# A twelve-layer transformer kernel on one core: the last layer's norms and residual, and the way attention's value sums are turned back

## What is computed

```
norm = maximum(linalg.norm(x, axis=-1), 1e-12);  rms_norm = x / norm * 128 ** 0.5 * gamma
light = gelu(rms_norm(x, light_gamma) @ light_w1 + light_b1) @ light_w2 + light_b2
s = einsum('bnd,d->bn', x, routing_token);  scores = coor_descent(s, k, 50 steps)
heavy = gelu(rms_norm(x, heavy_gamma) @ heavy_w1 + heavy_b1) @ heavy_w2 + heavy_b2
out = light + heavy * (score of the position, made of the descent)
```

## Time and profile before

| | |
|---|---|
| runs | 756.26, 756.54, 758.40 us; median 756.54 |
| the profiled execution | 757.45 us, span of its instructions 755.7 us |
| busy, share of the span | PE 79%, PEld 52%, DVE 64%, ACT 33%, POOL 16% |
| mean granted TensorE clock | 0.879 |
| the chain of work that ended last, share by engine | PE 70%, DVE 21%, POOL 4%, ACT 3%, issue 2% |
| attention's loops, five layers | turns of about 3.1 to 4.0 us, all on the chain that ended last |
| L3f, from L1106 of group 0 | 708.74 to 755.7 us |

### The profile page before, as it was taken

One profiled execution on the slowest core, in us unless ns is written; L12 is line 12 of the kernel. 1 busy time (PEld: TensorE's weight loads), 2 busy tenths in 40 slices (PEclk: granted clock), 3 DMA queues, 4 the chain that ended last, 5 costly groups with the idle time before them and its releaser, 6 DMA issues.

```text
span 755.7 us, 10867 instructions
## 1 busy us (share of the span) xinstructions
PE 597.1 (79%) x4297; PEld 392.8 (52%) x4305; DVE 485.1 (64%) x1288; ACT 245.6 (33%) x361; POOL 119.1 (16%) x118
## 2 busy tenths in 40 slices
PE   2314599976999899969977878998779869996486
PEld 1314255676455645656665755556435554564335
DVE  7788777677588666753354536785654547766685
ACT  2342134414334333334414332344221032443150
POOL 5023510014210131010010014200200061102110
PEclk9657579979899999987997799899799977999678
DMA  9600000000000000000000000000000000000000
GB/s 314 279 0 1 0 1 2 1 1 2 0 2 1 1 1 2 1 1 1 1 0 1 1 1 0 1 2 1 1 0 1 0 1 1 1 2 0 1 0 29
DMA packets 6722, 12.42 MB, mean 16 GB/s; under 512 B 528, under 2 KB 4880, under 8 KB 6288
## 3 DMA queue, kind: packets, MB, share of 16 engines
q1 hardware_dynamic: 6672, 11.73, 4.3%
HBM read 11.21 MB, written 0.52 MB: 16 GB/s over the span
## 4 chain that ended last, share of the span: by engine, by line
PE 70%; DVE 21%; POOL 4%; ACT 3%; issue 2%; POOLq 0%; DVEq 0%; ACTq 0%
PE ps L410 52%; PE ps L473 11%; PE ps L491 3%; PE ps L426 3%; DVE st L1106 2%; DVE xn L1278 2%; POOL rs L324 2%; DVE x L1208 1%; DVE mv L1109 1%; DVE big L1194 1%; DVE mx L1188 1%; ACT td L846 1%; PE ps L578 1%; ACT big L866 1%; PE ps L699 1%
## 5 line engine op out<-in xcount | busy, mean ns | idle before, releaser
L1188 DVE TENSOR_REDUCE mx<-ps 128x8 f32<-128x1024 f32 x80 | 98.0, 1225 | 60.9 <-PE ps L410 60.8
L866 ACT ACTIVATE big<-ps 128x1024 f32<-128x1024 f32 x80 | 81.9, 1023 | 139.7 <-PE ps L473 139.7
L1194 DVE TENSOR_TENSOR big<-ps,mx 128x1024 f32<-128x1024 f32 x80 | 97.7, 1221 | 4.3
L410 PE MATMUL ps<-KTm,qk 32*128 32x512 f32 x320 | 96.3, 682 | 0.0
L473 PE MATMUL ps<-kt,big 128*128 128x128 f32 x640 | 89.4, 285 | 4.6 <-DVE big L1194 4.5
L324 POOL TENSOR_TENSOR rs<-ve,negh 128x4 f32<-128x4 f32 x26 | 26.6, 1023 | 414.0 <-DVE ve L1111 414.0
L473 PEld LDWEIGHTS ps<-kt,big 128*128 128x128 f32 x640 | 72.6, 145 | 26.7 <-DVE big L1194 14.0
L410 PE MATMUL ps<-xnT,wt 128*128 128x512 f32 (+1 forms) x148 | 76.9, 658 | 3.1 <-DVE big L1467 3.1
L410 PE MATMUL ps<-wt,big 128*128 128x128 f32 (+1 forms) x480 | 61.0, 280 | 0.0
L410 PEld LDWEIGHTS ps<-wt,big 128*128 128x128 f32 (+1 forms) x480 | 56.4, 191 | 8.0 <-issue 6.0
L410 PEld LDWEIGHTS ps<-big,vaug 128*32 128x32 f32 x1280 | 30.4, 109 | 48.0 <-ACT big L866 30.3
(11 more groups left out here) (261 smaller groups left out, 790.9 us busy)
## 6 DMA issues: line engine op xcount, KB each, us to landing
wt<-in_weights SPq DMA_DIRECT2D x1, 1664.0 KB, 16.8
wt<-in_weights SPq DMA_DIRECT2D x1, 1603.0 KB, 11.5
wt<-in_weights SPq DMA_DIRECT2D x6, 256.0 KB, 10.6
bt<-in_bconsts SPq DMA_DIRECT2D x1, 1024.0 KB, 7.9
rowt<-in_rows SPq DMA_DIRECT2D x1, 975.0 KB, 5.5
wt<-in_weights SPq DMA_DIRECT2D x1, 832.0 KB, 13.0
wt<-in_weights SPq DMA_DIRECT2D x1, 608.0 KB, 18.1
wt<-in_weights SPq DMA_DIRECT2D x1, 580.0 KB, 5.7
```

The source lines that it names most:

```text
L410: return pe.matmul(out, lhsT, rhs, start=start, stop=stop, **k)
L866: act.activation(half, heads_of(pair(g, u)), ACT.Exp, scale=SCALES[l]).then_inc(*s.step(f"exp{u}"))
L1188: dve.tensor_reduce(top, S, AX.X, ALU.max).then_inc(*s.step())
L1194: dve.tensor_tensor(pr[:, half * HH:(half + 1) * HH, :].rearrange("p (i j) k -> p i j k", i=2), S, top.unsqueeze(3).to_broadcast([P, 2, HG ...
```

## The change

Two independent parts.

Attention: the value sums of each batch are copied to a tile of their own (`ot`: td, tc, xn, xnT), so that the next `weighted` waits only for that copy (OT). The transposes back of batches 0 to 2 move behind the loop, into three score banks (`EARLIER`: banks 1 to 3 for group 0, 4 to 6 for group 1), group 0 waiting for group 1's last exponential; that of batch 3 follows. VectorE divides the first three batches by one reciprocal and one multiplication over three banks (`normal`), and the last by two of the old size (`normal_last`).

Last layer, and the norm of L2f: the mean square of a normalised row is not summed from the row but computed from the layer norm's statistics, as variance times rs squared (`square_norm`, three 128x4 instructions after var_r), in L3f ahead of the routing scores. ScalarE multiplies the rows by the norm (xr). In L3f, TensorE adds x to the light product by a product with the identity (bank 1), the heavy bias is one product for all four batches, ScalarE copies bank 1 to `tc` (base), and VectorE's one scalar_tensor_tensor for each batch then gives x itself. The turn of f stands inside group 1's heavy products, ahead of batch 2. Group 1's last step has a phase behind group 0's.

```diff
 # tensor, attend
                     if half == 0 and b:
-                        pe.wait_ge(*s.at(f"{l}.co{b - 1}"))
+                        pe.wait_ge(*s.at(f"{l}.OT{b - 1}"))
...
                     for i in range(GB):
-                        ins = pe.transpose(VALUES[g][:, i * P:(i + 1) * P], t.td[:, i, :], ident)
+                        out = (VALUES[g] if b == GB - 1 else EARLIER[g][:, b, :])[:, i * P:(i + 1) * P]
+                        ins = pe.transpose(out, t.ot[b][:, i * P:(i + 1) * P], ident)
...
-                    if u >= 3 and u % 2 == 1:
-                        back(u // 2 - 1)
...
                 weighted(UNITS - 1)
+                yield n, beat(g, UNITS, 1)
+                if g == 0:
+                    pe.wait_ge(*s.at(f"{l}.exp{UNITS - 1}", 1))
+                for b in range(GB - 1):
+                    back(b)
                 yield n, beat(g, UNITS, 2)
                 back(GB - 1)
 # tensor, L3f
+                    pe.wait_ge(*s.at("L3f.xb"))
                     pe.wait_ge(*s.at("L3f.h4"))
+                    mm(bank(1), ident, x[:, :, :], stop=False, skip_group_check=True)
...
-                            mm(seq(2, b), hid[:, c, b * P:(b + 1) * P], w("L3f_hw2")[:, c * P:(c + 1) * P], start=c == 0, stop=False)
-                        ins = mm(seq(2, b), ones[0:1, :], row("L3f_hb2", 1), start=False)
+                    mm(bank(2), ones[0:1, :], row("L3f_hb2", 1).unsqueeze(1).to_broadcast([1, GB, P]), stop=False, skip_group_check=True)
+                    for b in range(GB):
+                        if g == GROUPS - 1 and b == 2:
+                            pe.wait_ge(*s.at("L3f.f"))
+                            pe.transpose(banks_of(0)(3)[:, 0:B], rt_e[:, :], ident[0:B, 0:B]).then_inc(*s.step("fT"))
...
 # scalar, L3f
+                    yield n, 3
+                    act.wait_ge(*s.at("L3f.xn"))
+                    act.wait_ge(*s.at("L3f.ms_r"))
+                    for b in range(GB):
+                        act.activation(tc[:, b, :], t.xn[:, b, :], ACT.Copy, scale=t.s4b[:, b:b + 1]).then_inc(*s.step("xr"))
                     if g == GROUPS - 1:
-                        yield n, 4
+                        yield n, 3.5
...
+                    yield n, 15
+                    read(tc[:, :, :], four(bank(1)), "light", "base")
 # vector
+            def square_norm(mul, add, op):
+                dve.wait_ge(*s.at(f"{s.layer}.var_r"))
+                dve.tensor_tensor(s4[:, 0:GB], t.rs[:, :], t.rs[:, :], ALU.mult).then_inc(*s.step())
+                dve.wait_ge(*s.last())
+                dve.tensor_tensor(s4[:, 0:GB], s4[:, 0:GB], t.mv[:, :, 1], ALU.mult).then_inc(*s.step())
+                dve.wait_ge(*s.last())
+                dve.tensor_scalar(s4[:, 0:GB], s4[:, 0:GB], mul, add, ALU.mult, op).then_inc(*s.step("ms"))
...
-                    if u >= 3 and u % 2 == 1:
-                        yield n, beat(g, u, 7.5 - 2 * g)
-                        normal(u // 2 - 1)
+                yield n, beat(g, UNITS, 2)
+                normal()
                 yield n, beat(g, UNITS, 3)
-                normal(GB - 1)
+                normal_last()
...
                 if l == "L3f":
+                    yield n, 1.5
+                    square_norm(1.0, 1e-24 / P, ALU.max)
...
-                    squares(xn)
-                    dve.tensor_scalar(s4[:, 0:GB], s4[:, 0:GB], 1e-24, None, ALU.max).then_inc(*s.step("ms"))
-                    yield n, 3
-                    dve.wait_ge(*s.at("L3f.ms_r"))
-                    dve.tensor_scalar(s4b[:, 0:GB], s4b[:, 0:GB], float(P) ** 0.5, None, ALU.mult).then_inc(*s.step())
-                    dve.wait_ge(*s.last())
-                    for b in range(GB):
-                        dve.tensor_scalar(tc[:, b, :], xn[:, b, :], s4b[:, b:b + 1], None, ALU.mult).then_inc(*s.step("xr"))
...
-                    yield n, 18
-                    dve.wait_ge(*s.at("L3f.xb"))
+                    yield n, 18 + g
+                    dve.wait_ge(*s.at("L3f.base"))
                     dve.wait_ge(*s.at("L3f.y"))
                     dve.wait_ge(*s.at("L3f.rf", GROUPS - 1))
                     for b in range(GB):
-                        dve.scalar_tensor_tensor(x[:, b, :], bank(2)[:, b * P:(b + 1) * P], rt_f[:, g * GB + b:g * GB + b + 1], x[:, b, :],
-                                                 ALU.mult, ALU.add).then_inc(*s.step())
-                    dve.wait_ge(*s.last())
-                    yield from add(n, l, 1)
+                        dve.scalar_tensor_tensor(x[:, b, :], bank(2)[:, b * P:(b + 1) * P], rt_f[:, g * GB + b:g * GB + b + 1], tc[:, b, :],
+                                                 ALU.mult, ALU.add).then_inc(*s.step("x"))
```

More of the change, by code:

```diff
@@ L151, in __init__ @@
             self.qT3 = qk[:, :].bitcast(BF16)[:, 0:3 * W4].rearrange("p (j n) -> p j n", j=3)
+            self.ot = [v[:, :, :].rearrange("p b d -> p (b d)") for v in (self.td, self.tc, self.xn)] + [self.xnT[:, :]]
             self.KTm = own("KTm", [P, 2, HG, P])
@@ L155, in __init__ @@
             self.mx, self.rc = own("mx", [P, 2, H // 2]), own("rc", [P, H])
+            self.rc3 = own("rc3", [P, GB - 1, H])
             self.co, self.coT = own("co", [P, GB, P]), own("coT", [P, W4])
@@ L178, in build @@
     PAIRS = (all_banks[:, 1:3, :], all_banks[:, 5:7, :], all_banks[:, 3:5, :])
+    EARLIER = (all_banks[:, 1:4, :], all_banks[:, 4:7, :])
     VALUES = tuple(all_banks[:, k, :] for k in (0, 7))
@@ L816, in program @@
                     yield n, 14
+                    pe.wait_ge(*s.at("L3f.xb"))
                     pe.wait_ge(*s.at("L3f.h4"))
+                    mm(bank(1), ident, x[:, :, :], stop=False, skip_group_check=True)
                     for b in range(GB):
-                        mm(seq(1, b), hid[0:HE2, 4, b * P:(b + 1) * P], w("L3f_lw2", HE2))
+                        ins = mm(seq(1, b), hid[0:HE2, 4, b * P:(b + 1) * P], w("L3f_lw2", HE2), start=False, stop=b == GB - 1, skip_group_check=True)
+                    ins.then_inc(*s.step("light"))
+                    mm(bank(2), ones[0:1, :], row("L3f_hb2", 1).unsqueeze(1).to_broadcast([1, GB, P]), stop=False, skip_group_check=True)
                     for b in range(GB):
+                        if g == GROUPS - 1 and b == 2:
+                            pe.wait_ge(*s.at("L3f.f"))
+                            pe.transpose(banks_of(0)(3)[:, 0:B], rt_e[:, :], ident[0:B, 0:B]).then_inc(*s.step("fT"))
                         for c in range(4):
-                            mm(seq(2, b), hid[:, c, b * P:(b + 1) * P], w("L3f_hw2")[:, c * P:(c + 1) * P], start=c == 0, stop=False)
-                        ins = mm(seq(2, b), ones[0:1, :], row("L3f_hb2", 1), start=False)
+                            ins = mm(seq(2, b), hid[:, c, b * P:(b + 1) * P], w("L3f_hw2")[:, c * P:(c + 1) * P], start=False,
+                                     stop=(c == 3 and b == GB - 1), skip_group_check=True)
                     ins.then_inc(*s.step("y"))
[L825 to L828, removed]
         weave(*(program(g) for g in range(GROUPS)))
@@ L875, in weighted_out @@
             def weighted_out(b, l):
-                if b:
-                    act.wait_ge(*s.at(f"{l}.OR{b - 1}"))
-                read(t.td[:, :, :], four(VALUES[g]), f"O{2 * b + 1}", f"OT{b}")
+                read(t.ot[b], VALUES[g], f"O{2 * b + 1}", f"OT{b}")
             for n, l in enumerate(LAYERS[1:STAGES + 1]):
@@ L1164, in attend, with normal, normal_last @@
             def attend(n, l):
-                def normal(b):
-                    dve.wait_ge(*s.at(f"{l}.OR{b}"))
+                def normal():
+                    dve.wait_ge(*s.at(f"{l}.OR{GB - 2}"))
+                    O = EARLIER[g].rearrange("p b (h d) -> p b h d", h=H)
+                    dve.reciprocal(t.rc3[:, :, :], O[:, :, :, HD]).then_inc(*s.step())
+                    dve.wait_ge(*s.last())
+                    dve.tensor_tensor(t.co[:, 0:GB - 1, :].rearrange("p b (h d) -> p b h d", h=H), O[:, :, :, 0:HD],
+                                      t.rc3[:, :, :].unsqueeze(3).to_broadcast([P, GB - 1, H, HD]), ALU.mult).then_inc(*s.step(f"co{GB - 2}"))
+                def normal_last():
+                    dve.wait_ge(*s.at(f"{l}.OR{GB - 1}"))
                     O = VALUES[g].rearrange("p (h d) -> p h d", h=H)
@@ L1169, in normal @@
                     dve.wait_ge(*s.last())
-                    dve.tensor_tensor(t.co[:, b, :].rearrange("p (h d) -> p h d", h=H), O[:, :, 0:HD],
-                                      wide(t.rc[:, :], HD), ALU.mult).then_inc(*s.step(f"co{b}"))
+                    dve.tensor_tensor(t.co[:, GB - 1, :].rearrange("p (h d) -> p h d", h=H), O[:, :, 0:HD],
+                                      wide(t.rc[:, :], HD), ALU.mult).then_inc(*s.step(f"co{GB - 1}"))
                 if l in ("L0x", "L1a", "L3a"):
@@ L1195, in attend, with add @@
```

(15 more changed lines are left out.)

3 lines of the change are left out of this document (1 added, 2 removed).

## The result

The changed kernel took 747.43 us (median of four runs, 746.02 to 748.75) against 757.04 for the kernel before on the same chip: ratio 0.9871, interval 0.9847 to 0.9895. The forecast was 745.5 from 756.54, a ratio of 0.985, within a range of 741.8 to 749.5. The profiled execution took 747.51, its span is 745.7 instead of 755.7.

The account below looks back on a forecast made before the run. TensorE's instructions and the waits between its bursts were taken to set the time. Attention -5.2 and L3f -5.8 (-3.3 + 0.33 - 2.85) gave -11.0 us: median 745.5 from 756.54, range 741.8 to 749.5.

Parts of the forecast that it names:

- The transposes' price and the slots: Attention loops: four transposes back cost 0.43 us, so slots of 3.52 become 3.09; six groups make 2.6 us per layer.
- Nothing but the order changes up to E: Attention loop up to the start of group 1's last exponential (E): only order changes, so it comes 2.6 us earlier.
- The tail: Attention behind the start of the last exponential: group 1's `co` is turned at 6.66 instead of 5.09 us, 1.57 longer.
- The net term: Attention per layer: 2.6 us gained less 1.6 lost, 1.03 net (0.5 to 1.3); 5.2 in five layers (2.5 to 6.5).
- L3f's start: Last layer: cheaper norm and row products on ScalarE start TensorE's long burst 3.3 us earlier (2.0 to 3.9).
- The burst: TensorE's long run of products in L3f: 0.33 us longer, with the turn of f some 0.2 and not waiting.
- The end: L3f behind the last product: group 1's four steps need 1.25 us where x took 4.1, so 2.85 less.
- The second: L3f's burst doesn't start earlier, ScalarE's products or the bias additions holding its queue: 3.3 us missing, 748.8; chance 10%.
- the fifth: Attention loops keep their pace while tails grow 1.6 us each, 8 lost against L3f's 5.8: 758.7; chance 5%.
- the fourth: Attention tails: moved transposes and their wait put TensorE at 1.2 GHz, slower, 761.5 us; chance 3%.
- The first: Attention tail takes all: moved transposes and divisions stay exposed, attention nets nothing, only L3f counts: 750.7 us; chance 12%.
- The third: TensorE's clock rises earlier: 1.3 us in L3f's burst and as much in attention's tails, 742.9 us; chance 12%.

Follow-up runs that it names:

- The gap filled with one batch: Changed kernel with only group 1's transposes back of batch 1 moved ahead of its last turn of scores; ratio 0.9818 to the kernel before.
- the run with the products on VectorE: Kernel before with the norms from statistics (L2f and L3f) alone, the eight row products staying on VectorE; ratio 0.9992 to the kernel before.
- the filled gap: Changed kernel with group 1's transposes back of batches 1 and 2 moved ahead of its last turn of scores; ratios 0.9813 and 0.9764 to the kernel before.
- the run with three divisions: Changed kernel with three pairs of divisions of the old size per group instead of one pair over three banks; ratio 0.992 to the kernel before.

## Why the prediction was right

**The transposes' price and the slots.** Right: 3.09 in the slots that had 3.03 to 3.58, and 2.6 us of transposes taken out of the loop.

**"Nothing but the order changes up to E."** This is the step that failed, and with it the term of 2.6 us. That VectorE and ScalarE don't fill a slot was read from full slots. Group 0's last slot has no scores of a next unit; it holds only `turned` and `weighted`, 1.6 us from 669.26, while VectorE's maximum and subtraction for group 1's last unit, 1.23 each, run from 668.80 to 671.36. The loop gains 2.07 per layer instead of 2.6 (read in L1a and L1x, whose loops run at a granted clock of 1.00 in both traces). In the kernel before, those transposes covered the wait. The gap filled with one batch gives 0.43 back.

**The tail.** 1.57 forecast, 1.62 to 1.63 measured in all five layers; reciprocal and product at the interpolated 0.46 and 0.56. The net term was 1.03 per layer and is 0.45 (0.43 to 0.46): 2.2 us in five layers instead of 5.2, below my lower bound of 2.5, since that was made of the new instructions' prices and knew no wait in the loop.

**L3f's start.** Forecast 3.3 (2.0 to 3.9), measured 4.1: 10.47 behind the statistics instead of 14.60. The term was mis-sized, above all at ScalarE's price: 2.45 for eight, near the lower row of the two, where I took the middle (2.8). ScalarE also starts 6.54 behind the statistics, where the forecast had 6.81. The wait behind GpSimd's additions did not come: the additions began (713.74) as the last routing score ended; smin has a 0.55 wait and is early enough.

**The burst.** Forecast 0.33 longer, measured about 0.25 shorter (716.69 to 741.71). The heavy products without bias products between them run closer: thirty-two in a row take 3.67 us, where they took four times 1.09, and group 0's y takes 6.84 (727.58 to 734.42) instead of 7.10 (734.35 to 741.45), 0.26 less where the sum had 0.06 more. The turn of f waits for nothing and costs some 0.3, not 0.2: from the sixteen products ahead of it (737.52) to those behind it (739.66) pass 2.14 us, and half of the thirty-two is 1.84. The clock, which rises 0.4 earlier in the burst, gives 0.1: the first twenty products take 10.89 instead of 11.01.

**The end.** 2.85 forecast; from the last product to the last x 1.2 instead of 4.1, so 2.9. Right. From there to the end of the span, with the store, it is 2.8 instead of 3.0.

**The sum.** Attention 2.2 instead of 5.2, L3f 7.5 instead of 5.8: 9.7 of the 10.0 between the two spans; the remaining 0.3 I put down to the clock, which gave here and took there. The two errors, 3.0 and 1.7, had different signs, so the sum is nearer than its terms: the total was right partly by luck, while the mechanism held in all but the one wait and the sign of the burst's small term. The two parts alone took 1.9 and 6.2 us off, 8.1 of the 9.6 that the medians of the whole change differ by; the traces of these parts show the same loops and tails, and the last layer to half a us, so this rest lies in the clock too or in the noise, which no run here separates.

**The rivals.** The second (the burst doesn't start earlier) and the fifth (slots as before) are out by the trace. So is the fourth: from the last exponential to the second addition the granted clock is 1.00 in all five layers, before and after. The first (the tail takes all) is nearer to the truth than the forecast was for attention, for a reason that it did not name. The third (the clock gives more) came to little in the burst: the clock rises 3.3 us behind its start instead of 3.7, which is 0.1 and not 1.3; its other half, in attention's tails, can't be, as the clock is 1.00 there already. The wait of VectorE behind GpSimd was seen in the run with the products on VectorE: 3.34 us for eight beside GpSimd's additions. The page "SBUF — State Buffer" of the Trainium skill, section "SBUF: two separate sides", says that of a VectorE instruction that needs the shared ports and a GpSimd one the later is held up for the whole of the earlier, and for GpSimd's large additions this trace agrees. For the routing scores beside the 128x4 powers, none of the traces shows a delay.

**Open.** What part of the 6.7 us of the filled gap is luck of where the clock changes, and whether that holds for other inputs or chips, I didn't settle: two sets of runs gave 741.93 and 739.57.

## What to carry to other kernels

When work leaves a steady loop, look at its first and last turns too: they have less of one engine's work, and what leaves may have covered another engine there. Work that is put behind a loop is exposed on every engine it touches; fill with it the waits that the loop's end has before adding to the tail, which was worth 0.43 to 0.56 us in each of five layers here. And a step from one engine to another (the row products) can be worth as much as a cheaper formula, when the old engine meets a third one at that time.

## What the runs showed of the hardware that was not expected

The granted clock moves a layer's length by more than most edits. L1x with the same matmuls was 74.34 us at a granted clock of 1.00, and 78.10 at 0.96 in the run with three divisions, of which 0.5 is that edit's. L0x was 94.85 and 91.01 long in the same two traces, at 0.82 and 0.87. Here is L1x of the run with three divisions, the five us up to the fall of the clock and five at 0.50:

```profile
262.17:267.17 5.00, 3.27 (x18) 1.53 (x17) 3.43 (x3) 0.99 (x2) 2.41 (x3) 1.00 0.01 3
268.00:273.00 5.00, 5.00 (x18) 2.65 (x16) 2.40 (x3) 0.44 (x1) 1.04 (x1) 0.50 0.00 0
```

And the changed kernel at the same place of L1x as the first row:

```profile
266.45:271.45 5.00, 3.27 (x18) 1.53 (x17) 3.42 (x3) 0.99 (x2) 2.42 (x3) 1.00 0.01 3
```

TensorE was busy for 3.27 of the five us in both, with the same instructions; in one the clock then falls, in the other it stays at 1.00. What decides between them, these traces don't show. So an effect of half a us per layer can be read only in a trace, or between kernels with many runs.
